# Softmax sums inverted through DRAM and maxima turned by VectorE, in a one-core attention and expert layer

## The reference, cut to what matters

```python
# x: (4, 512, 128); 16 heads of 64 share one key and one value head
xn = layernorm(layernorm(x), g1, b1)
q = xn @ Wq;  k, v = split(xn @ Wkv)
sim = (q * 64 ** -0.5) @ k.T              # per head: 512 x 512
attn = exp(sim - rowmax) / rowsum
x = x + layernorm((attn @ v) @ Wo, g2, b2)
x = x + moe(layernorm(x))                 # 8 experts, the best 2 of each token, gate/up/down with gelu
```

## Time and profile before

| what | value |
|---|---|
| median of 3 runs | 621.04 us (620.53 to 622.22) |
| the profiled execution: time, span | 620.37 us, 618.6 us |
| mean granted TensorE clock | 0.98 |
| busy: TensorE, VectorE, GpSimd, ScalarE | 579.3, 388.5, 395.4, 307.1 us |
| attention, with the constants and loads ahead of it | to about 467 us |
| change-over to the experts | 467 to 500 us |
| expert tiles and the end | 500 to 618.6 us |

### The profile page before, as it was taken

The page is one execution under the profiler, slowest core; times in us unless marked ns, Lnnn a source line. Parts: engine busy times, 40 slices in busy tenths (PEclk is TensorE's granted clock), DMA queues, the critical chain, the costliest instruction groups (busy, mean ns, idle before and its releaser), DMA issues. The chain is left out here.

```text
span 618.6 us, 8866 instructions
## 1 busy us (share of the span) xinstructions
PE 579.3 (94%) x2611; PEld 330.1 (53%) x2611; DVE 388.5 (63%) x792; ACT 307.1 (50%) x576; POOL 395.4 (64%) x329
## 2 busy tenths in 40 slices
PE   8799999999999998998999989999997979999990
PEld 6464555444554454454545535444443567888880
DVE  4967557656646878584567786975384468444443
ACT  2345646455546554463556445545635553455540
POOL 5457677658668855598598558959745934354331
PEclk9999999999999999798999999999999999999996
DMA  5111012010101200061000000000004400230005
GB/s 162 69 70 70 2 70 73 1 69 3 72 24 48 73 0 2 6 229 76 2 2 3 1 2 17 23 1 2 12 1 123 118 22 27 67 94 29 21 16 204
DMA packets 26990, 29.46 MB, mean 48 GB/s; under 512 B 7523, under 2 KB 18021, under 8 KB 26944
## 3 DMA queue, kind: packets, MB, share of 16 engines
q1 hardware_dynamic: 24672, 24.66, 12.3%
q0 software_dynamic: 2272, 4.24, 2.1%
HBM read 13.50 MB, written 15.32 MB: 47 GB/s over the span
## 5 line engine op out<-in xcount | busy, mean ns | idle before, releaser
L1134 ACT ACTIVATE prob<-s_ps 128x512 f32<-128x512 f32 x256 | 150.5, 598 | 177.0 <-PE s_ps L1240 175.1
L1058 DVE TENSOR_REDUCE rowmax<-max_ps 128x1 f32<-128x512 f32 x256 | 174.2, 690 | 101.4 <-PE max_ps L1209 99.1
L989 POOL TENSOR_TENSOR fold<-prob 128x1024 f32<-128x1024 f32 x63 | 149.8, 2377 | 94.5 <-ACT prob L1134 93.9
L1254 PE MATMUL pv_ps<-prob,v 128*64 128x512 f32 x512 | 139.0, 623 | 0.0
L1238 PE MATMUL s_ps<-q_hl,khh 128*128 128x512 f32 x256 | 118.5, 463 | 0.6 <-ACT prob L1134 0.6
L1209 PE MATMUL max_ps<-khh,q_hl 128*128 128x512 f32 x256 | 103.3, 409 | 7.7 <-DVE rowmax L1058 3.9
L1240 PE MATMUL s_ps<-q_hm,kly 65*128 65x512 f32 x256 | 102.3, 400 | 0.0
L1238 PEld LDWEIGHTS s_ps<-q_hl,khh 128*128 128x128 f32 x256 | 48.9, 191 | 79.5 <-ACT prob L1134 59.8
L995 POOL TENSOR_TENSOR psums<-fold 128x512 f32<-128x512 f32 x63 | 82.3, 1306 | 4.9
L1209 PEld LDWEIGHTS max_ps<-khh,q_hl 128*128 128x128 f32 x256 | 49.1, 192 | 27.3 <-DVE rowmax L1058 11.2
L1240 PEld LDWEIGHTS s_ps<-q_hm,kly 65*128 65x128 f32 x256 | 49.0, 191 | 8.9 <-issue 3.4
(11 more groups left out here) (230 smaller groups left out, 767.2 us busy)
## 6 DMA issues: line engine op xcount, KB each, us to landing
sorted_rows<-raw_w SPq DMA_DIRECT2D x36, 260.0 KB, 2.6
raw_w<-in_gate_upT SPq DMA_DIRECT2D x8, 512.0 KB, 8.3
wd<-in_downT SPq DMA_DIRECT2D x8, 256.0 KB
raw_w<-parts SPq DMA_DIRECT2D x8, 256.0 KB, 3.9
psums<-sorted_rows SPq DMA_DIRECT2D x22, 65.0 KB, 1.9
x<-in_x SPq DMA_DIRECT2D x4, 256.0 KB, 4.1
out<-x SPq DMA_DIRECT2D x4, 256.0 KB, 2.3
xs_first<-sorted_rows SPq DMA_DIRECT2D x15, 65.0 KB, 2.2
```

Source lines behind the costliest of these rows:

```text
L989: nc.gpsimd.tensor_tensor(fold[:, :, :], prob[:, head % 4, 0:2, :], prob[:, head % 4, 2:4, :], ALU.add).then_inc(prob_folded, 1)
L1058: nc.vector.tensor_reduce(rowmax[:, group % 2, it, i:i + 1], max_ps[:, k % 2, :], AX_X, ALU.max).then_inc(max_done, 1)
L1134: nc.scalar.activation(prob[:, head % 4, jt, :], s_ps[:, k % 2, :], ACT.Exp, scale=SCALE).then_inc(exp_done, 1)
L1254: last = nc.tensor.matmul(pv_ps[DH * hd:DH * hd + DH, :], v[:, b % 2, jt, :], prob[:, head % 4, jt, :], start=(jt == 0), stop=(jt == JT - 1))
```

## The change: what it does

1. RECIP is one reciprocal. GATHER writes `rinv` (16 KB) to a DRAM tensor. A new step CAST (slot 10.5 of a unit) waits on SP until that has landed, and issues two DMAs, one for each side of 64 partitions. Each reads a unit's reciprocals 64 times over from DRAM: 512 KB each, into `over_sum`, [128, 4, 512] in SBUF. NORM is then only VectorE's product of `over_sum` and `raw`. The matmuls with `headsel`, their constants, GpSimd's copies of those and four small input DMAs are gone.
2. The maximum is written negated; SHIFT is four VectorE transposes of 32 x 32 into `mrow`, now [32, 2, 128]. TensorE's transposes and ScalarE's copy are gone. The DMAs to `q_hm` move the same bytes from 8 partitions each.
3. In the change-over SP issues `wd` 0 and 1, the rows of tile 2, GATHER, `wd` 2 to 7, then CAST, then the rows from tile 3 on. VectorE does the four NORMs in a row behind `hidden(1)`; TensorE does `gate(2)`, `up(2)`, `turn_hidden(0)` and then the four OUTs.

```diff
 def tail_vector(dve, kind, u, a):
     if kind == "RECIP":
         dve.wait_ge(spread_in, 32 * (u + 1))
-        link(dve, nc.vector.reciprocal(rinv[:, :], spread[:, :]))
         if u >= 1:
-            dve.wait_ge(rhl_in, 32 * u)
-        link(dve, nc.vector.tensor_copy(halves[:, 0, :], rinv[:, :]))
-        nc.vector.tensor_tensor(halves[:, 1, :], rinv[:, :], halves[:, 0, :].bitcast(F32),
-                                ALU.subtract).then_inc(recip_done, 1)
+            dve.wait_ge(recips_out, 16 * u)
+        nc.vector.reciprocal(rinv[:, :], spread[:, :]).then_inc(recip_done, 1)
     if kind == "NORM":
         k = u * UP + a
-        dve.wait_ge(norm_mm, k + 1)
+        dve.wait_ge(over_sum_in, 32 * (u + 1))
         dve.wait_ge(raw_ready, k + 1)
 ...
-        nc.vector.tensor_tensor(ao[:, k % 2, :], sum_ps[:, :], raw[:, k % RAW_SLOTS, :],
+        nc.vector.tensor_tensor(ao[:, k % 2, :], over_sum[:, a, :], raw[:, k % RAW_SLOTS, :],
                                 ALU.mult).then_inc(ao_ready, 1)
 # tail_sync
     if kind == "GATHER":
         sp.wait_ge(recip_done, u + 1)
+        sp.dma_start(recips[u].rearrange("(p c) -> p c", c=SPREAD), rinv[:, :]).then_inc(recips_out, 16)
+    if kind == "CAST":
+        sp.wait_ge(recips_out, 16 * (u + 1))
         if u >= 1:
-            sp.wait_ge(norm_mm, u * UP)
-        else:
-            sp.wait_ge(consts_set, 1)
-        for part in range(2):
-            sp.dma_start(rhl[part * LOW_ROW:part * LOW_ROW + UH, :].bitcast(F32),
-                         halves[:, part, :].bitcast(F32)).then_inc(rhl_in, 16)
+            sp.wait_ge(ao_ready, u * UP)
+        of_heads = recips[u].rearrange("(c h q) -> h c q", h=2, q=S)
+        for hd in range(2):
+            sp.dma_start(over_sum[DH * hd:DH * hd + DH, :, :],
+                         of_heads[hd].unsqueeze(0).broadcast_to([DH, UP, S])).then_inc(over_sum_in, 16)
 # tail_tensor
-    if kind == "NORM":
-        k = u * UP + a
-        pe.wait_ge(rhl_in, 32 * (u + 1))
-        if k >= 1:
-            pe.wait_ge(ao_ready, k)
-        nc.tensor.matmul(sum_ps[:, :], headsel[:, a, :], rhl[:, :], start=True,
-                         stop=True).then_inc(norm_mm, 1)
 # VectorE, attention
-    nc.vector.tensor_reduce(rowmax[:, group % 2, it, i:i + 1], max_ps[:, k % 2, :], AX_X,
-                            ALU.max).then_inc(max_done, 1)
+    nc.vector.tensor_reduce(less_max[:, group % 2, col:col + 1], max_ps[:, k % 2, :], AX_X,
+                            ALU.max, negate=True).then_inc(max_done, 1)
+if kind == "SHIFT":
+    head, heads = shift_heads[u]
+    group = head // 4
+    dve.wait_ge(max_done, (head + heads) * JT)
+    if u >= 2:
+        rows_came(dve, u - 2)
+    for n in range(P // 32):
+        part = slice(32 * n, 32 * n + 32)
+        last = nc.vector.transpose(mrow[:, u % 2, part].bitcast(F32),
+                                   less_max[part, group % 2, :].bitcast(F32))
+    last.then_inc(mrow_ready, 1)
 # SP, change-over
-for k in range(EARLY_ROWS, LIST_TILES[0]):
-    if k == EARLY_ROWS + 1:
-        tail_sync(sp, "GATHER", last_unit)
-    if k - EARLY_ROWS < E // 2:
-        load_down(2 * (k - EARLY_ROWS))
-        load_down(2 * (k - EARLY_ROWS) + 1)
+load_down(0)
+load_down(1)
+load_rows(sp, EARLY_ROWS, rows(EARLY_ROWS))
+tail_sync(sp, "GATHER", last_unit)
+for e in range(2, E):
+    load_down(e)
+tail_sync(sp, "CAST", last_unit)
+for k in range(EARLY_ROWS + 1, LIST_TILES[0]):
     load_rows(sp, k, rows(k))
```

More of the change, by code:

```diff
@@ L86, in attention_schedule @@
                 place(after + RECIP_AT[n], 5, kind, u, 0)
+            place(after + CAST_AT, 5, "CAST", u, 0)
             for c in range(UP):
@@ L117 @@
 RECIP_AT = (6, 6, 9, 9)
+CAST_AT = 10.5
 SUM_AT = (-7, 5)
 LAST_SUM_AT = (-7, 4)
-LAST_STEPS = (("SUMS", 0), ("SPREAD", 0), ("RECIP", 0), ("GATHER", 0), ("NORM", 0), ("NORM", 1), ("OUT", 0),
+LAST_STEPS = (("SUMS", 0), ("SPREAD", 0), ("RECIP", 0), ("GATHER", 0), ("CAST", 0), ("NORM", 0), ("NORM", 1), ("OUT", 0),
               ("NORM", 2), ("OUT", 1), ("NORM", 3), ("OUT", 2), ("OUT", 3))
@@ L811, in bass_preln_mqa_moe_kernel @@
         last_pv = max(n for n, step in enumerate(steps) if step[0] == "PV")
-        tail_steps = [step for step in steps[last_pv:] if step[0] in ("RAW", *RECIP_STEPS, "NORM", "OUT")]
+        tail_steps = [step for step in steps[last_pv:] if step[0] in ("RAW", *RECIP_STEPS, "CAST", "NORM", "OUT")]
         assert all(step in tail_steps or step[0] in ("PV", "SUM") for step in steps[last_pv:])
@@ L883, in _ @@
                 sp.dma_start(wof[:, :, :], wo.rearrange("(c p) n -> p c n", p=P)).then_inc(wo_in, 16)
[L884 to L888, removed]
                 for b in range(1, NB):
@@ L971, in _ @@
                         if k == 0:
-                            link_pool(pool, nc.gpsimd.memset(headsel[:, :, :].bitcast(F32), 0.0))
-                            link_pool(pool, nc.gpsimd.memset(rhl[:, :].bitcast(F32), 0.0))
-                            pool.wait_ge(hs_in, 64)
-                            for part in range(2):
-                                held = slice(part * LOW_ROW, part * LOW_ROW + UH)
-                                nc.gpsimd.tensor_scalar(headsel[held, :, :], hs_raw[held, :, :], 1.0, 1.0, ALU.mult,
-                                                        ALU.mult).then_inc(headsel_set, 1)
-                                pool.wait_ge(headsel_set, part + 1)
                             set_constants(pool)
@@ L1168, in _ @@
                         keep_busy(BUSY[kind])
-                    if kind in ("XT", "K", "V", "Q", "SHIFT", "YT", "X3T", "LOGIT", "RANK") and (kind, u) not in (("K", 0), ("SHIFT", 0)):
+                    if kind in ("XT", "K", "V", "Q", "YT", "X3T", "LOGIT", "RANK") and (kind, u) != ("K", 0):
                         if in_bank:
@@ L1210, in _ @@
                                          khh[:, b % 2, :], start=True, stop=True).then_inc(max_mm, 1)
-                    if kind == "SHIFT":
-                        head, heads = shift_heads[u]
-                        pe.wait_ge(max_done, (head + heads) * JT)
-                        group, i = divmod(head, 4)
-                        for t in range(TPB):
-                            last = nc.tensor.transpose(shift_bank(u)[0:heads, t * P:(t + 1) * P],
-                                                       rowmax[:, group % 2, t, i:i + heads],
-                                                       ident[:, :])
-                        last.then_inc(shift_mm, 1)
                     if kind == "EXP":
@@ L1457, in _ @@
                 low_gate_up(dve, 1, wl_ready)
-                tail_vector(dve, "NORM", last_unit, 0)
                 low_gate_up(dve, 2, wl_ready)
-                tail_vector(dve, "NORM", last_unit, 1)
                 hidden(1)
-                tail_vector(dve, "NORM", last_unit, 2)
-                tail_vector(dve, "NORM", last_unit, 3)
+                for c in range(UP):
+                    tail_vector(dve, "NORM", last_unit, c)
                 hidden(2)
@@ L1616, in up, with keep_busy @@
                     times(up_ps[:, k % 2, :], k, F).then_inc(up_mm, 1)
-                def keep_busy(times):
-                    for _ in range(times):
-                        nc.tensor.matmul(ht_ps[:, :], headsel[:, 0, :], headsel[:, :, :].rearrange("p k c -> p (k c)"),
-                                         start=True, stop=True)
-                keep_busy(4)
+                def keep_busy(width):
+                    nc.tensor.matmul(ht_ps[:, 0:width], ident[:, :], wof[:, 0:width // P, :].rearrange("p k c -> p (k c)"),
+                                     start=True, stop=True)
+                keep_busy(S)
                 turn_in(0)
-                keep_busy(2)
+                keep_busy(S // 2)
                 for e in range(E):
@@ L1636, in _ @@
                 turn_in(2)
-                tail_tensor(pe, "NORM", last_unit, 0)
                 gate(2)
-                tail_tensor(pe, "NORM", last_unit, 1)
-                tail_tensor(pe, "OUT", last_unit, 0)
-                tail_tensor(pe, "NORM", last_unit, 2)
+                up(2)
                 turn_hidden(0)
-                tail_tensor(pe, "OUT", last_unit, 1)
-                tail_tensor(pe, "NORM", last_unit, 3)
-                up(2)
-                tail_tensor(pe, "OUT", last_unit, 2)
-                tail_tensor(pe, "OUT", last_unit, 3)
+                for c in range(UP):
+                    tail_tensor(pe, "OUT", last_unit, c)
                 turn_hidden(1)
```

53 lines of the change are left out of this document (23 added, 30 removed).

## The result

The changed kernel took 654.2 us (median of 4 runs, 651.7 to 660.6), the kernel before 621.6 us on the same chip (620.5 to 625.8): ratio 1.0515, 95% interval 1.0454 to 1.0575. The direction was as forecast, the size was not: 627 us with a range up to 636.

A forecast was written before the change was run, and what follows sets the result against it. TensorE, busy 94% of the span, was taken as the bound. 620.4 us less 11.4, plus 0.7, 7.0, 3.5 and 6.5, gave 626.7; with the median's 0.7 shift, 627 us. Range 613.5 to 636, the forecast's own 623 to 631.

The forecast's parts named there:

- the term of 7.0 us for `mrow` behind the casts: Attention: first EXP of the next four heads waits for `mrow` behind 1 MB, 1.0 us per cast, seven casts, 0 to 10.
- a rival at 4 us: Half-speed clock behind idle TensorE stretches: 2 us each in some two places, within a 634 us case, chance 0.20.
- The wait's size: Attention, first EXP of the next four heads: stall of 1.4 us at 204 GB/s, none at 408; taken as 1.0 us.
- my half rate: Casts filling 64 partitions run at 204 GB/s: the megabyte takes 5.1 us, `mrow` lands at 106.0, stall 1.4 us.
- The clock: Granted clock 0.50 behind an idle TensorE stretch, also in front of OUT: 2 us each in some two places.
- half rate and the clock: Rival: stalls of 1.5 us or more a unit (+3 us) plus half clock, 2 us in some two places; 634 us, chance 0.20.
- VectorE in NORM: VectorE's wait in NORM 14 holds the following maxima; two PSUM buffers cover about 3 us, so nothing added.
- TensorE's work: Attention: removed NORM matmuls save 6.4 us and 15 steady SHIFTs 5.0 us, together 11.4 us; bounds 8 to 12.5.
- Transposes: VectorE's four transposes a SHIFT: 0.2 us for one, 0.8 us a SHIFT, beside TensorE in steady attention.
- The start: Two SHIFTs lie where VectorE makes TensorE wait: +0.7 us, 0 to 1.6.
- NORM of two SBUF operands: Attention: NORM beside GpSimd's fold delays a maximum, 0.45 us in seven units, 0.3 for routing units; +3.5 us, 0 to 9.
- The change-over: Casts behind `wd`, then four NORMs and OUT: TensorE's order 4 to 9 us later, 11 at half rate; net +6.5 us.

## Why the prediction was wrong, point by point

**The step that failed** is the term of 7.0 us for `mrow` behind the casts, and the lower clock behind the waits, which the sum put at nothing and a rival at 4 us. In their place: 16.5 us of TensorE's waits, and about 16 us of clock (377.08 against 360.75 busy us for the same matmuls; 14.4 by the run with filling products). That is 33 us in the changed kernel where the sum had 7. Of it 27.3 us came back when the casts had a quarter of their size, since other waits of TensorE were longer there.

- **The wait's size.** I had 1.4 us at half rate and took 1.0. In the unit of the earlier trace rows it was 2.10. Counted from the spread's issue, the rows came in at 14.9 us (90.50 to 105.44) and not at 14.05, and the reader was ready at 12.84, as forecast within 0.2 us. The casts were issued at 7.15 us, 0.5 sooner than forecast, and their flow, at 226 to 229 GB/s, was faster than the 204 of my half rate. What the sum lacked is the time between the end of the flow and the reader, about 1.3 us in the unit at 327.98: I counted bytes over rate and no landing behind it. In the last unit the wait was 3.5 us, though the rows came 14.8 us after the spread's issue, since their reader was ready at 11.3 us. That I went below the half rate's 1.4 "because nothing shows one half filled at full speed" was the wrong way to read a missing row. The Trainium skill's figure for 64 partitions, in "SBUF — State Buffer", section "Door 1: The DMA port swizzle", led to an estimate of 10.5 us. The rate here was 226 to 229 GB/s against its 196, and the waits were larger still, since they were not bandwidth alone.
- **The clock.** I priced it from one stretch at 2 us, in two places. The windows show it behind five of the seven waits for `mrow` and behind three others; the mean clock of attention fell from 0.99 to 0.94. The rival "half rate and the clock" (634 us, chance 0.20) had the mechanism and a quarter of its price.
- **VectorE in NORM.** In the changed kernel VectorE waits 30.8 us for `over_sum` in attention and TensorE only 4.5 for its maxima: I was right that little of it shows. But it was hidden by TensorE's own wait for `mrow`. Take that away and it shows (31.8 us of TensorE's waits for maxima in attention with the NORMs at their old slots). With these slots the two are one lateness seen by two engines, and the order of the queue alone doesn't give it back.
- **TensorE's work.** Right for the transposes: 5.0 us forecast, 4.0 shorter and 6.5 busy us less when done alone. The 6.4 us for the NORM products were not measured by themselves; the run with small casts has both savings, 7.7 busy us less at a clock lower by 0.01, and a stretch of only 2.0 us less.
- **Transposes** at 0.2 us: 0.198. The start: +0.7 us forecast, 1.5 us less measured up to the first spread.
- **NORM of two SBUF operands.** +3.5 us forecast. L731 took 30.1 us busy in 32 instructions, up to 2.4 us each, but its middle one 0.70 us; TensorE's wait for maxima in attention went from 1.9 to 4.5 us. The term was about right, if it is the cause; no run takes it away alone.
- **The change-over.** CAST was issued 4.0 us after GATHER (3.7 forecast) and NORM started 10.4 us after CAST (9.8 at half rate). `turn_hidden(1)` was 11.1 us later in its order, my upper end, and nothing was given back behind it: some +11.8 where the sum had +6.5. `wd` ahead of the casts is 5 us of it.

## What to carry to other kernels

A small transfer that an in-order engine needs stands behind whatever is issued ahead of it on the queue; price the large one at the rate of its own shape, and if no row shows that shape, take the slow end. Count the landing behind the last byte too. Where TensorE is the bound and never idle, the price of a short stall in each unit can be twofold, the wait and the half clock behind it. When a datum is late, moving another ahead of it in the queue can just change who waits: with `mrow` first VectorE stood in NORM at its old slots, and TensorE behind its maxima; at later slots less of that was seen, but the slots and the later issue cost 14.8 us by themselves. Fewer bytes or a higher rate gave most of the time back, and the half of the change that needs neither, the transposes on VectorE, is the one to keep in the kernel before (0.6%).

## What the hardware showed that I had not expected

- Two casts of 512 KB into 64 partitions each ran at 209 to 229 GB/s, on one queue or on two at once (226 over 4.5 us); the same megabyte into 128 partitions by one DMA at up to 362 (328 over 3 us).
- A DMA whose source's slowest dimension is 2 kept two of 16 DMA engines busy (share 0.13) at 51 GB/s, and made the kernel 26% slower.
- The granted clock fell to half behind a TensorE wait of 1.15 us and not behind one of 2.10 us.
- Ten filling products ahead of a wait made the kernel faster (ratio 1.032 against 1.0515), though they do no work.
